# The delta loop's hand-over from tile to tile, eight tiles a turn, and an earlier norm in the window attention

## The reference

```python
qkvz = x @ W_in                                   # q, k, v, z: 16 heads of 64
qkv  = silu(conv1d_causal(qkv, conv_w, taps=4))
beta, g = sigmoid(b), -A * softplus(a + dt_bias)  # from x @ W_ba
q, k = l2norm(q) * HD ** -0.5, l2norm(k)
def step(S, (qt, kt, vt, gt, bt)):                # along each sequence of 256
    S = S * exp(gt)
    S = S + outer(kt, (vt - kt @ S) * bt)
    return S, qt @ S
y = norm_w * rmsnorm(y) * silu(z)
x = x + y @ W_o
```

## Time and profile before

| | |
|---|---|
| median of 3 runs | 6117.34 us (6099.32 to 6126.91) |
| profiled execution | 6087.45 us, of which the span is 6085.7 |
| PE busy | 5156.0 us, 85% |
| DVE busy | 3611.1 us, 59% |
| ACT busy | 2854.3 us, 47% |
| POOL busy | 2789.0 us, 46% |
| mean granted TensorE clock | 0.930 |

### The profile page before, as it was taken

How to read it: one execution, slowest core, us unless ns; L and a number is a source line. 1 busy time by engine, 2 the same in 40 slices (tenths; PEclk the granted TensorE clock), 3 DMA queues, 4 the chain that set the end, 5 groups by cost and what they waited for, 6 DMA issues and landing times. The chain is left out here.

```text
span 6085.7 us, 206341 instructions
## 1 busy us (share of the span) xinstructions
PE 5156.0 (85%) x78381; PEld 3866.5 (64%) x78382; DVE 3611.1 (59%) x6984; ACT 2854.3 (47%) x5746; POOL 2789.0 (46%) x3045
## 2 busy tenths in 40 slices
PE   4899999999999999999999776688887899994496
PEld 3666666666666666666666555566665666663496
DVE  6666666666666666666666664544444666664443
ACT  1555555555555555555555413333332455451175
POOL 5766666666666666666666533400001000005453
PEclk9999999999999999999999988899898999995598
DMA  3000000000000000000000103200000000001124
GB/s 111 20 25 25 24 25 25 23 24 23 25 25 24 25 24 25 24 25 25 24 25 25 39 20 65 66 1 0 0 0 2 1 0 0 0 0 54 36 70 128
DMA packets 126297, 167.29 MB, mean 27 GB/s; under 512 B 33016, under 2 KB 110880, under 8 KB 123052
## 3 DMA queue, kind: packets, MB, share of 16 engines
q1 hardware_dynamic: 94924, 123.07, 6.7%
q0 software_dynamic: 14080, 26.64, 1.3%
q10 hardware_dynamic: 16640, 8.39, 0.7%
HBM read 118.84 MB, written 105.69 MB: 37 GB/s over the span
## 5 line engine op out<-in xcount | busy, mean ns | idle before, releaser
L934 PE MATMUL bank<-wc,shifted 128*128 128x512 f32 (+1 forms) x2344 | 1055.9, 570 | 19.0 <-issue 15.7
L1324 ACT ACTIVATE TT<-bank 128x512 bf16<-128x512 f32 x640 | 374.0, 595 | 540.7 <-PE bank L1060 289.4
L934 PEld LDWEIGHTS bank<-wc,shifted 128*128 128x128 f32 x2344 | 403.6, 194 | 299.3 <-issue 287.0
L1411 POOL TENSOR_TENSOR qa<-qa,qt 128x512 f32<-128x512 f32 x390 | 487.7, 1272 | 34.8 <-POOL qt L1406 34.8
L1406 POOL TENSOR_TENSOR qt<-qp,cq 128x256 f32<-128x256 f32 x780 | 474.6, 639 | 23.2 <-POOL qa L1411 23.2
L1089 PE MATMUL bank<-X,kqe 64*64 64x64 f32 x12480 | 447.1, 221 | 24.7 <-DVE rb L1593 19.6
L1640 DVE TENSOR_TENSOR yb<-bank,masks 128x512 bf16<-128x512 f32 x512 | 352.0, 687 | 185.6 <-PE bank L1041 185.6
L1089 PEld LDWEIGHTS bank<-X,kqe 64*64 64x64 f32 x12480 | 399.7, 134 | 71.1 <-issue 52.5
L1324 ACT ACTIVATE T<-bank 128x512 bf16<-128x512 f32 x512 | 287.1, 595 | 252.4 <-PE bank L1053 250.4
L3280 DVE TENSOR_REDUCE mxp_full<-bank_full 128x2 f32<-128x512 f32 x524 | 325.7, 685 | 108.7 <-PE bank_full L3029 108.7
L1041 PEld LDWEIGHTS bank<-T,mTb 128*128 128x128 bf16 x5120 | 202.7, 97 | 253.1 <-ACT T L1324 81.1
(11 more groups left out here) (547 smaller groups left out, 12974.1 us busy)
## 6 DMA issues: line engine op xcount, KB each, us to landing
sent_l0f<-blank_l0f SPq DMA_DIRECT2D x64, 528.0 KB
sent_l1m<-blank_l1m SPq DMA_DIRECT2D x64, 528.0 KB
xin<-sent_l1m SPq DMA_DIRECT2D x139, 66.0 KB
taken_l1m<-back_l1m SPq DMA_DIRECT2D x16, 512.0 KB, 8.7
xin<-sent_l0f SPq DMA_DIRECT2D x75, 66.0 KB
x_sb<-in_L_attn_x_dram SPq DMA_DIRECT2D x32, 128.0 KB, 2.9
cw_stage<-in_L_attn_conv_w_dram SPq DMA_DIRECT2D x4, 1024.0 KB, 6.5
x_rows<-x_sb ACTq DMA_DIRECT2D x8, 512.0 KB, 11.8
```

The source lines that it names most:

```text
L934: mm = pe.matmul(bk[:, cols], src[:, j, :], w["wc"][:, j, at * 512 + cols.start:at * 512 + cols.stop], start=(j == 0), stop=(j == TAPS - 1 ...
L1324: nc.scalar.activation(dst, bk[:, :].rearrange("p (h a u) -> p h a u", h=8, u=1 << l), ACT.Copy).then_inc(actb.done.sem, 1)
L1411: ins = pool.tensor_tensor(qa[:, H, :], qa[:, H, :], qt[:, H, :], ALU.add)
```

## The change

Six edits. A turn of the delta loop has eight tiles, two groups of sequences, so that half as many branches are taken; `goes_on(t)` tells a tile with state, `carried(t)` counts those. GpSimd's convolution waits for both masked halves (`tt_ready`). VectorE's `add_out` stands between the two halves. The copy of the odd columns (`odd_columns`) and the queries' silus stand ahead of z's second silu in level 5. In the stateless tile `scale_k` stands there too. And in the window attention `norm_h` stands ahead of `add_out`.

```diff
-    U = STEPS
+    U = 2 * STEPS
+    def goes_on(t):
+        return t > 0 and t % STEPS > 0
+    def carried(t):
+        return t // STEPS * (STEPS - 1) + t % STEPS
...
             with pool.Fori(0, turns) as b:
                 for t in range(U):
+                    lone_wait(pool, tt_ready.sem, tt_ready.at(b, NB * (t + 1)), pool_passed)
                     convolve(b, t + 1)
...
                 product(3)
-                first_level(b, t + 1)
+                first_level(b, t + 1, 0)
                 add_out(b, t)
-            def first_level(b, f):
+                first_level(b, t + 1, 1)
+            def first_level(b, f, s):
                 dve.wait_ge(mb_ready.sem, mb_ready.at(b, NHB * (f + 1)))
-                for s in range(NB):
-                    dve.tensor_tensor(TT[f % 2][of(s), :, of(s)], mTb[of(s), :, of(s)],
+                dve.tensor_tensor(TT[f % 2][of(s), :, of(s)], mTb[of(s), :, of(s)],
...
+            def odd_columns():
                 dve.tensor_copy(T[:, :, 1:P:2], c["identb"][:, 1:P:2].unsqueeze(1).to_broadcast([P, H0, HALF]))
...
                             if (l, G) == (LEVELS - 1, 1):
+                                silu_q(b, t + 1)
+                                odd_columns()
+                                if not goes_on(t):
+                                    scale_k(b, t)
                                 silu(b, "z1", z2)
-                        if l == 4:
-                            silu_q(b, t + 1)
...
                     squares_by_token(b, t + 1)
-                    scale_k(b, t)
+                    if goes_on(t):
+                        scale_k(b, t)
...
+            def norm_next(b, u):
+                if u == 0:
+                    dve.wait_ge(scales_ready.sem, scales_ready.at(b, 1))
+                norm_h(b, u // TPB + 2, am_use(u - 1, "hT") if u else 4)
...
                     maxima(b, 0)
+                    if window and t == 0:
+                        norm_next(b, u)
                     add_out(b, u, u)
                     if t == 0:
                         values(b, 1 - p)
-                        if u == 0:
-                            dve.wait_ge(scales_ready.sem, scales_ready.at(b, 1))
-                        norm_h(b, turn + 2, am_use(u - 1, "hT") if u else 4)
+                        if not window:
+                            norm_next(b, u)
```

More of the change, by code:

```diff
@@ L751, in dve_slot @@
             names += [f"a.{l}.0", f"{step}.0", f"a.{l}.1", f"{step}.1"]
-        state = t > 0
+        state = goes_on(t)
         names += ["s.0", "s.1"] * state + ["sq"]
@@ L832, in delta_attention @@
         k_ready = signal("k_ready", U)
-        kd_ready = signal("kd_ready", U - 1)
+        kd_ready = signal("kd_ready", carried(U))
         rows_in = [signal(f"decay_rows_in{t}", 16 * LOADS * U // TPB) for t in range(TPB)]
@@ L837, in delta_attention @@
         mb_ready = signal("mb_ready", NHB * U)
-        rhs_ready = signal("rhs_ready", U - 1)
-        S_ready = signal("S_ready", U - 1)
+        rhs_ready = signal("rhs_ready", carried(U))
+        S_ready = signal("S_ready", carried(U))
         rhsb_ready = signal("rhsb_ready", U)
@@ L885, in kd_of @@
         def kd_of(b, t):
-            return kd_ready.sem, kd_ready.at(b, t % U + 1 + t // U * (U - 1))
+            return kd_ready.sem, kd_ready.at(b, carried(t) + 1)
         @block.sync
@@ L1011, in decayed @@
                 turn_heads(b, k2, "k")
-                done = 2 if t > 0 else 0
+                done = 2 if goes_on(t) else 0
                 taps(b, src, "k1", done, 4 - done)
@@ L1192, in _ @@
                     decay(b, t, 1)
-                    if t > 0:
+                    if goes_on(t):
                         from_state(b, t, 0, "ks")
@@ L1310, in right_side @@
             def right_side(b, t):
-                if t == 1:
+                if t % STEPS == 1:
                     proj.was_done(act, b, t - 1, "v1")
                 else:
-                    act.wait_ge(rhs_ready.sem, rhs_ready.at(b, max(t - 1, 0)))
+                    act.wait_ge(rhs_ready.sem, rhs_ready.at(b, carried(max(t - 1, 0))))
                 nc.scalar.activation(rb[:, :, :], v2[:, :, :], ACT.Copy).then_inc(rhsb_ready.sem, 1)
@@ L1461, in decayed @@
                 gate_o(b, t)
-                if t != U - 2:
+                if t % STEPS != STEPS - 2:
                     f = bass.ds(b * U + t + 1, 1) if t >= 0 else slice(0, 1)
-                    if t > 0:
+                    if goes_on(t):
                         lone_wait(pool, dveb.full.sem, dveb.full.at(b, dveb.uses.at(t, "s.1")), pool_passed)
@@ L1595, in correct @@
                     ins = dve.tensor_tensor(X[:, hs, :], X[:, hs, :], bk, ALU.add)
-                elif t != 1:
+                elif t % STEPS != 1:
                     ins = dve.tensor_tensor(o[:, hs, :], o[:, hs, :], bk, ALU.add)
@@ L1659, in _ @@
                             silu(b, "v1", v2)
-                    if t > 0:
-                        dve.wait_ge(S_ready.sem, S_ready.at(b, t - 1))
+                    if goes_on(t):
+                        dve.wait_ge(S_ready.sem, S_ready.at(b, carried(t - 1)))
                         for s in range(NB):
@@ L3489, in delta_stage @@
                         x_all, mr, gates, decay_rows, tiles, (beside_sync, blank_last, beside_pool))
-        delta_attention(nc, c, {"wc": wc, "wq": wq, "cq": cq, "wz": wz, "wo": wo}, x_all, mr, gates, decay_rows, tiles // STEPS,
+        delta_attention(nc, c, {"wc": wc, "wq": wq, "cq": cq, "wz": wz, "wo": wo}, x_all, mr, gates, decay_rows, tiles // (2 * STEPS),
                         sendings)
```

10 lines of the change are left out of this document (5 added, 5 removed).

## The result

| | before | changed |
|---|---|---|
| median | 6121.17 us (6099.32 to 6126.91, 4 runs) | 5942.61 us (5928.67 to 5967.03, 4 runs) |
| span of the profiled execution | 6085.7 us | 5935.9 us |
| mean granted TensorE clock | 0.930 | 0.935 |

The ratio is 0.9719, with a 95% interval from 0.9678 to 0.976. The medians differ by 178.6 us, the two profiled executions by 149.5, for the profiled execution of the kernel before (6087.45 us) was faster than any of its timed runs.

The account below looks back on a forecast made before the run. TensorE was taken to bound the delta loop, over half the span, so only its idle time or low clock could yield gains. Terms 67.2 + 10.6 + 6.4 + 27.2 = 111.4 us gave ratio 0.9817, median 6005 us, range 5965 to 6055.

Parts of the forecast that it names:

- the window attention's term: Window attention: norm_h ahead of add_out lets TensorE turn h 0.85 us sooner, 32 times: 27.2 us, bounds 16 and 46.
- the clock as a rival: TensorE's clock falls less: delta loop gains at least 14 us, window attention some more, about 5985; chance 0.14.
- The delta loop's term: Delta loop: hand-overs 67.2, fewer branches 10.6 and stateless tiles 6.4 us; forecast 84.2 us.
- The wait for `out`: Delta loop hand-overs inside a turn: earlier add_out frees the bank, saving TensorE 1.40 us 48 times, 67.2 us.
- Eight tiles a turn: Delta loop branches: 8 of the hand-overs at a branch become plain, each saving the 1.33 us stop, 10.6 us.
- The stateless tile: First of each four delta tiles: earlier scaled keys, partly given back by z's later silu; 0.4 us 16 times, 6.4 us.
- GpSimd behind the halves: Delta loop: convolution waits for the second masked half; ScalarE's wait of about 1 us stays hidden; nothing taken, bound 11 us.
- this sign of being wrong: Stateless tile: z's later silu would make kd or the scaling of z later.
- the unlikely side: Delta loop: clock falling in every tile instead of once in four would lose 42 us, 6047; shared chance 0.20.
- GpSimd as the bound: Delta loop: GpSimd's lateness holds ScalarE's tanh of the queries, making the kernel slower, about 6166; chance 0.04.
- half given back: TensorE meets other waits sooner, losing half the delta gain, window attention at its lower bound: about 6060; shared chance 0.20.
- no change: Delta loop: the wait for out merely hid another, only some 20 us remain, 6095 to 6117; chance 0.06.

Follow-up runs that it names:

- e2: Kernel before, with TensorE filling its window-attention wait for h with four unread identity products, order unchanged: 6030.77 us, ratio 0.9925.
- e6: Kernel before with add_out moved between the two masked halves and nothing else: 6020.02 us, ratio 0.9921.
- e5: Changed kernel with four tiles a turn again (16 turns): 5953.57 us, ratio 0.9801 to the kernel before.
- e12: Changed kernel with the queries' squares products widened to 128 columns and the stateless tile's scale_k back in its old place: 5900.3 us, ratio 0.9713.
- e7: Changed kernel with the sixteen products of the queries' squares moving 128 columns instead of 16: 5874.86 us, ratio 0.9685 to the kernel before.
- e11: Kernel before with only the queries' squares products widened from 16 to 128 columns: 6039.69 us, ratio 0.994.
- e1: Kernel before with only the window attention's norm moved ahead of add_out: 6012.8 us, ratio 0.9875.

## Why the prediction was wrong, point by point

**The step that failed** is the window attention's term, "32 x 0.85 = 27.2 us". Its mechanism was right and the order gave 22.4 to 27 us. Missing from the sum, and so put at nothing, was what the same 1.44 us of idle time did to the clock: with it the stage spent 155 us at half clock, without it 20. e2 shows the two apart, 59.8 us for the clock against 22.4 for the order. The stage gave 82.2 us, 55 more than its term. With these 55 the sum is 166 us, and by the prediction's own ratio the median about 5950, against 5942.6 measured. The text had the clock as a rival, at 5985 and a chance of 0.14, and was right about the side ("less idle time means fewer falls"), but priced only the delta loop's falls (14 us) and passed over the attention with "some more". The trace of the kernel before had it: a mean clock of 0.90 over 754 us, and 155 us at half clock, more than twice the delta loop's 68. The rule cited there (the Trainium skill, "TensorE: Matmul & The Clock Gate", section "What's actually happening") says that activity releases the throttle. e2 agrees: with TensorE active in the wait, the stage's clock went from 0.90 to 0.98.

**The delta loop's term**, 84.2 us, measured 79.1. That they are so near is partly luck: the change was worth 91.3 at a steady clock, and the clock took some 12 back. By parts:

- The wait for `out`: 67.2 forecast, some 71 by e6 after its falls are priced. The 2.74 us from `a.0.0` to the join came out to the hundredth; the tile after the branch was a good model.
- Eight tiles a turn: 10.6 forecast, 9 by e5 after the same correction.
- The stateless tile: 6.4 forecast, for all that stands there. The waits of TensorE in it fell from 1.12 + 0.65 to 1.14, 0.63 us a tile or 10 us, and e12 puts `scale_k` alone at 0.73. The term was too small: z's product on GpSimd begins 2.96 us later, counted from the first join, where 3.1 to 3.56 were forecast, for the copy took 0.74 us there and not 1.04. The wait for z grew because TensorE, no longer held by the keys, comes to it sooner; in e12, where the keys are late again, it is 0.65. Counted from the first join, the turning of z itself comes sooner (35.69 us after it, 36.42 before), so this sign of being wrong did not appear.
- The column copy and the queries' silus: hidden, as forecast, as far as the traces show; VectorE's idle time before the state's sum shrank from 3.45 to 1.62 us. They were not run alone.
- GpSimd behind the halves: nothing was lost, as forecast, and nothing won either. ScalarE waits the forecast microsecond at hT and TensorE does not notice.

**The clock in the delta loop** went the way that I had priced as the unlikely side and had named as a sign of being wrong: 26 falls instead of 16. The prediction looked to the idle time of the stateless tile before each fall. The idle time did not decide it, for the change removed idle time there and the falls grew in number; and all 16 falls of the kernel before began 2.0 to 2.9 us after the first of the sixteen narrow products had started. They ended when these were widened (e7, and e11 on the kernel before), a stretch in which TensorE is busy. Why the better order met that stretch more often was not tried by itself. The count differed between kernels (16, 19, 24, 25, 26, 34, 37) and even between executions of one loop: e2 has the delta loop of the kernel before and had 19 falls, where the kernel before and e1 had 16.

**The rivals.** GpSimd as the bound, half given back, and no change are all refuted: no wait for GpSimd appeared on TensorE's list, and the longest waits that were there before kept their length (15.0, 11.6, 6.1 and 4.5 us for `T`, `last`, `rb` and `yb` before, 14.5, 11.6, 6.1 and 4.5 after). Only the wait for z grew clearly, from 0.65 to 1.14 us.

## What to carry to other kernels

Price a stall of TensorE twice: its length, and what the granted clock of the stage says beside it; in the window attention here, at a mean clock of 0.90 with a stall in every pair of tiles, the second was 59.8 us and the first 22.4. A tile in which the suspected wait happens not to bind, here the one behind the loop's branch, can be a good model of the tile without that wait. An order that costs nothing to a neighbour (GpSimd's wait here) may make two instructions faster and gain nothing: ask who waits for them.

## What the runs showed of the hardware that was not expected

- Products that nobody reads, in a wait of 1.44 us every 20.8, took 59.8 us off a stage of 754 (e2); the granted clock went from 0.90 to 0.98.
- TensorE can be busy all along and still be given the lower level of 1.2 GHz: the delta loop of 64 tiles had 16 to 37 falls of the clock, all 222 of nine kernels within 1.96 to 3.46 us of the start of sixteen products of 16 columns, and 128 columns in place of 16 (275 ns each instead of 263) ended it in five kernels.
- A fall cost a tile with state 1.1 to 1.3 us, and the count of falls is no fixed property of a loop: the same delta loop had 16 in two executions, once in each turn of four tiles, and 19 in a third.
